# The backward bias of a relational graph layer: from the projections to the last means

## The chip, the cores and the metric

The kernel runs on one core of one Trainium2 chip. The metric is the time of one execution on the device in microseconds. The engines of the core are TensorE (PE; its weight loads are listed apart as PEld), VectorE (DVE), ScalarE (ACT), GpSimd (POOL) and SyncE (SP), which work side by side and wait for one another through semaphores.

## The reference

Two graph layers are applied to 3125 nodes of 256 features with 100000 edges: first an edge network with a gate (L0), then a relational layer (L1) with 16 relations, whose messages run along the edges and, with weights of their own, against them. The change concerns L1:

```
def _typed_pass(feat, W, bias, src_idx, dst_idx, etypes, norm_per_edge, n):
    proj = jnp.einsum('ni,rio->rno', feat, W)
    m = proj[etypes, src_idx] + bias
    m = m * norm_per_edge[:, None]
    return segment_sum(m, dst_idx, num_segments=n)
...
norm_f = _inv_degree(dst, n)[dst]
m_forward = _typed_pass(feat, Wf, forward_bias, src, dst, etypes, norm_f, n)
norm_b = _inv_degree(src, n)[src]
m_backward = _typed_pass(feat, Wb, backward_bias, dst, src, etypes, norm_b, n)
s = feat @ loop_weight
s = s + s + self_bias
return s + m_forward + m_backward
```

Since the norm of an edge is one over the number of edges of its node, each pass is a mean over a node's edges. The mean of a bias that is the same for all edges is the bias itself where the node has an edge, and 0 where it has none.

## The kernel before

Nodes lie in 25 blocks of 128 (`NB`), edges in 196 steps of 512 (`ST`, four columns of 128 edges). The program of each engine is written out by hand, in the order in which it runs; loops are hardware loops with 48 steps in a body.

**L0** (until some 1500 us of the profiled execution) computes the edge network step by step. Its second layer takes its bias by a product of ones with `bias_k` (`core_bias`, line 631), whose rows are made ready by `split_row` (lines 901 to 907).

**Forward projections** (some 1500 to 1812 us): relation pairs `q` = 0 to 7 multiply all 25 node blocks by two relations' weights. `project` (lines 766 to 778) makes six products of 128x512 for a block into one of five PSUM slots, ACT copies the slot (`evacuate`, line 264) and SP stores it to the table `proj` in HBM (line 325).

**The middle stage** (some 1867 to 3025 us) does two things at once. PE alternates between `project` for a block of the pairs 8 to 15, the backward weights (line 812), and `sum_projections` for a step of the forward sum (line 816). For the sum, POOL gathers four times 128 rows of `proj` per step (`gather_rows`, line 425) into one of eight buffers (`gbuf`), DVE compares the edges' nodes with the numbers of a node block (`one_hot`, line 1001), PE multiplies the two (line 679) and DVE adds the product to `acc` (`add_sums`, line 1034). Where a step's edges reach into further blocks, PE and DVE do a further round for each (lines 697 and 1025 to 1040). POOL may fill a buffer again when PE has reported the step that read it by `s_agg[1]` (line 434). In the first half of the stage DVE also sorts the edges by source (lines 1217 and 1220). In this stage alone `project` starts with a product of ones with the backward bias, which so stands in each projected row (lines 771 to 773).

**Between the stages** POOL waits until the last projection is stored (line 440), and DVE takes the forward means (`mean`, line 1279) and adds the forward bias (`forward_bias`, line 1284), times `some`, which is 1 for a node with edges and 0 otherwise. `fbias_p` is in PSUM.

**The last stage** (some 3027 to 4207 us) gathers from the backward projections into twelve buffers and sums by source over two blocks at once (`sum_backward`, line 721; `compare2`, `add2`, line 1058).

**The end**: `backward_mean` takes one over the number of edges and then 25 means, each of which reports to `s_final`; SP stores six blocks at a time, and the last 53 rows alone (lines 364 to 369).

Of the kernel before, what the change touches and what calls it, by code (L numbers as in the profile page):

```python
# [12 lines left out]
P = 128  # L13
# [13 lines left out]
NW = 12  # L27
# [24 lines left out]
def gnn_program(nc, x, dst_l, src_l, typ_l, ea_t, W1, b1, W2, b2, Wg, bg, gamma, beta,  # L52
# [9 lines left out]
    with ctx:  # L62
# [23 lines left out]
        bias_k = sb("bias_k", [P, 2, H], F32R)  # L86
# [3 lines left out]
        brow, gamma_b, beta_b = rows_a[:, 0:2 * H], rows_a[:, 2 * H:3 * H], rows_a[:, 3 * H:4 * H]  # L90
        rows_b = sb("rows_b", [P, 4 * H])
# [29 lines left out]
        bias_raw = fa[0:2, 6144:6144 + 2 * H].rearrange("p (d f) -> p d f", d=2)  # L121
# [104 lines left out]
        s_ones = sem("s_ones")  # L226
        s_xagg = [sem(f"s_xagg{k}") for k in range(3)]
# [67 lines left out]
        def _(sp):  # L295
# [66 lines left out]
            for n in range(5):  # L362
                sp.wait_ge(s_pst[n], 16 * 5 * NQ)
            for b in range(0, NB - 1, OB):
                sp.wait_ge(s_final, b + OB)
                sp.dma_start(out[b * P:(b + OB) * P, :].rearrange("(b p) f -> p b f", p=P), res[:, b:b + OB, :]).then_inc(s_out, 16)
# [81 lines left out]
        def _(act):  # L448
# [22 lines left out]
            for d, bias in enumerate((b2, bbias)):  # L471
                act.dma_start(bias_raw[:, d, :], bias.to_broadcast([2, H])).then_inc(s_w, 16)
# [115 lines left out]
        def _(pe):  # L588
# [177 lines left out]
            def project(q, u, b, d):  # L766

                n = b % 5
                if b >= 5 or past(q, 1):
                    pe.wait_ge(s_pev[n], 5 * q + b // 5)  # L770
                if d:
                    nc.tensor.matmul(pslots[n].rearrange("p (r f) -> p r f", r=2), ones_k[:, :],
                                     bias_k[:, 1:2, :].to_broadcast([P, 2, H]), start=True, stop=False)
                for m, (a, c) in enumerate(PARTS):
                    for kk in range(HK):
                        last = nc.tensor.matmul(pslots[n], hT[:, a, kk, b * P:(b + 1) * P], wsp[:, u, c, kk, :],  # L776
                                                start=(not d and m == 0 and kk == 0), stop=(m == 2 and kk == HK - 1))
                last.then_inc(s_proj, 1)

            def forward_relations(i):  # L780
                for u in range(2):
                    pe.wait_ge(s_wlo, 2 * i + u + 1)
                    for b in range(NB):
                        project(2 * i + u, u, b, 0)

            for g in range(NB // GB):
                for b in group(g):
                    transposes(1, b)
                if g == 0:
                    pe.wait_ge(s_wlo, 1)  # L790
                for b in group(g):
                    pe.wait_ge(s_hT[1], b + 1)
                    project(0, 0, b, 0)
            pe.wait_ge(s_wlo, 2)
            for b in range(NB):
                project(1, 1, b, 0)
# [9 lines left out]
            with pe.Fori(0, NQ // 4) as i:  # L806
                for u in range(2):
                    q = 2 * i + NQ // 2 + u
                    pe.wait_ge(s_wlo, q + 1)
                    project(q, u, 0, 1)  # L810
                    for m in range(QS):
                        project(q, u, m + 1, 1)
                        t = QS * u + m
                        if m % GS == 0:
                            w = windows_of(pe, 0, 2 * QS * i + GS + t, GS)
                        sum_projections(1, 2 * QS * i + GS + t, (GS + t) % RF, 2 * QS // RF * i + (GS + t) // RF, w[m % GS])
# [11 lines left out]
        def _(dve):  # L828
# [458 lines left out]
            def backward_mean():  # L1287

                inverse_degrees()
                for b in range(NB):  # L1290
                    mean(b, s_final)
# [107 lines left out]
```

## Time and profile before

| | us |
|---|---|
| median of 3 runs | 3757.14 |
| lowest, highest | 3756.84, 3758.55 |
| span of the profiled execution | 4225.8 |

The profiled execution is 468.7 us longer than the median of the runs. A row of a view is one group of instructions with its busy time and count; behind the bar or in square brackets is the time in which the engine sat idle just before them and what ended it. "issue" is idle time for which the profile shows no wait; "remote" is a wait whose end the profile cannot assign to an instruction. Starts of PE instructions are recorded, their ends are modelled.

### The profile page before, as it was taken

How to read it: one execution, taken by the hardware profiler on the slowest of the kernel's cores; microseconds unless marked ns; L12 is line 12 of the kernel's file. 1: busy time of each engine (PE TensorE's matmuls, PEld its weight loads, DVE VectorE, ACT ScalarE, POOL GpSimd, SP SyncE). 2: the span in 40 equal slices, each digit the busy share in tenths (PEclk: the TensorE clock that was granted, in tenths of full speed). 3: DMA queues.
4: the chain of work that ended last, by engine and by line, in shares of the span. 5: the costliest groups of instructions: out<-in, count | busy, mean ns of one | idle time of the engine just before them, and what ended most of it. 6: DMA issues, size and time to landing. Idle time of an engine off the chain costs nothing.

```text
span 4225.8 us, 72762 instructions
## 1 busy us (share of the span) xinstructions
PE 3453.7 (82%) x21136; PEld 2922.2 (69%) x21137; DVE 2451.8 (58%) x3368; ACT 984.1 (23%) x1538; POOL 2535.0 (60%) x3139
## 2 busy tenths in 40 slices
PE   6999999999999969966767777676668777778787
PEld 5989999989899958855555555565546565566655
DVE  6888888888888888845555532222423333333334
ACT  3444444544444444400111011001100000000000
POOL 2777777777777600046666666656566666666663
PEclk8999999999999989978888888889878888888888
DMA  5655655555555536634444464444333333333332
GB/s 166 171 168 163 171 169 163 168 163 166 164 165 161 153 106 204 207 120 134 141 140 141 126 148 141 138 128 133 103 90 91 89 87 87 88 88 92 92 91 80
DMA packets 322754, 569.98 MB, mean 135 GB/s; under 512 B 73896, under 2 KB 218392, under 8 KB 322584
## 3 DMA queue, kind: packets, MB, share of 16 engines
q0 software_dynamic: 137984, 411.19, 34.6%
q1 hardware_dynamic: 182732, 154.33, 11.4%
q10 hardware_dynamic: 1868, 2.52, 0.2%
q8 instruction: 67, 1.10, 0.1%
q14 instruction: 103, 0.84, 0.1%
HBM read 452.43 MB, written 115.41 MB: 134 GB/s over the span
## 4 chain that ended last, share of the span: by engine, by line
PE 47%; another core or an unknown queue 18%; issue 13%; DVE 12%; DVEq 7%; ACT 1%; POOL 1%; DMA 0%; POOLq 0%; ACTq 0%
PE pc L669 12%; PE pa L679 10%; PE pu L659 4%; DVE key L1220 4%; PE pg L643 4%; DVE tops L1217 3%; PE pu L651 3%; PE pu L721 3%; PE pa L721 2%; PE pg L721 2%; DVEq L277 2%; PE pu L776 1%; PE pg L776 1%; DVE fa L1001 1%
## 5 line engine op out<-in xcount | busy, mean ns | idle before, releaser
L406 POOL DMA_INDIRECT fa<-ptab,slot x784 | 814.1, 1038 | 348.8 <-issue 185.8
L425 POOL DMA_INDIRECT hr<-proj,row_dst x784 | 746.8, 953 | 427.6 <-issue 216.3
L425 POOL DMA_INDIRECT fa<-proj,row_src x400 | 381.5, 954 | 566.1 <-DMA proj<-fa 342.8
L669 PE MATMUL pc<-ws,hr 128*128 128x256 f32 x4704 | 614.4, 286 | 8.3 <-issue 6.7
L669 PEld LDWEIGHTS pc<-ws,hr 128*128 128x128 f32 x4704 | 577.3, 190 | 15.9 <-issue 15.0
L721 PE MATMUL pu<-hr,fa 128*128 128x258 f32 x1056 | 322.1, 441 | 134.5 <-issue 104.8
L679 PE MATMUL pa<-fa,onehot 128*128 128x256 f32 x904 | 252.3, 430 | 160.6 <-DVE onehot L1001 77.7
L721 PEld LDWEIGHTS pu<-hr,fa 128*128 128x128 f32 x1056 | 226.2, 217 | 214.7 <-issue 152.6
L1034 DVE TENSOR_TENSOR acc<-acc,pa 128x256 f32 x196 | 82.3, 420 | 465.9 <-remote 270.0
L679 PEld LDWEIGHTS pa<-fa,onehot 128*128 128x128 f32 x904 | 188.7, 214 | 213.4 <-issue 139.4
L721 PE MATMUL pg<-hr,fa 128*128 128x258 f32 x1040 | 301.0, 440 | 42.0 <-issue 39.2
L721 PEld LDWEIGHTS pg<-hr,fa 128*128 128x128 f32 x1040 | 231.2, 225 | 106.9 <-issue 64.1
L1001 DVE SCALAR_TENSOR_TENSOR fa<-pc,base,src_f 128x1024 f32<-128x1024 f32 (+1 forms) x210 | 261.6, 1247 | 74.7 <-issue 66.0
L505 ACT ACTIVATE hr<-pu 128x512 fp32r<-128x512 f32 x392 | 213.0, 596 | 303.1 <-PE pu L659 181.3
L516 ACT CAST hr<-fa 128x1024 fp32r<-128x1024 f32 x196 | 205.9, 1051 | 320.7 <-DVE fa L1008 249.4
L985 DVE SCALAR_TENSOR_TENSOR hr<-pu,hr 128x1024 fp32r<-128x1024 f32 x196 | 238.8, 1218 | 61.7 <-ACT hr L505 55.8
L721 PE MATMUL pa<-hr,fa 128*128 128x258 f32 x1040 | 252.4, 392 | 16.5 <-issue 15.2
L1008 DVE TENSOR_TENSOR fa<-fa,pc 128x1024 f32<-128x1024 f32 x196 | 238.1, 1215 | 44.2 <-PE pc L669 31.8
L776 PE MATMUL pu<-hr 128*128 128x512 f32 x960 | 256.1, 410 | 6.5 <-issue 5.2
L679 PE MATMUL pa<-hr 128*128 128x258 f32 (+1 forms) x1760 | 250.3, 285 | 11.6 <-issue 8.6
L1014 DVE TENSOR_TENSOR hr<-fa,hr 128x1024 fp32r<-128x1024 f32 x196 | 241.9, 1234 | 22.6 <-ACT hr L516 4.9
L425 POOL DMA_INDIRECT ws<-proj,row_src x192 | 181.5, 945 | 113.3 <-issue 52.1
(162 smaller groups left out, 5813.7 us busy)
## 6 DMA issues: line engine op xcount, KB each, us to landing
proj<-fa SPq DMA_DIRECT2D x400, 256.0 KB
fa<-in_ea_t SPq DMA_DIRECT2D x196, 128.0 KB
fa<-ptab,slot POOLq DMA_INDIRECT x784
hr<-proj,row_dst POOLq DMA_INDIRECT x784
fa<-in_Wrel SPq DMA_DIRECT2D x32, 256.0 KB
ptab<-fa SPq DMA_DIRECT2D x25, 256.0 KB, 2.0
fa<-proj,row_src POOLq DMA_INDIRECT x400
ws<-proj,row_src POOLq DMA_INDIRECT x192
```

Source lines behind the costliest of these rows:

```text
L406: pool.indirect_dma_start(pbuf[:, n % 2, j, :], None, ptab[:, :], bass.IndirectOffsetOnAxis(ap=slot[:, n, j:j + 1], axis=0)).then_inc(s_ga ...
L425: pool.indirect_dma_start(buffer[:, j, 0:H], None, table, bass.IndirectOffsetOnAxis(ap=rows[:, J * s + j:J * s + j + 1], axis=0)).then_inc ...
L505: last = nc.scalar.activation(uT[:, par, 0, h, :, :].rearrange("p k e -> p (k e)"), pu[:, h, :], ACT.Relu)
L516: nc.scalar.copy(msg[:, par, 0, :, :], gate[:, par, :, :]).then_inc(s_mhi, 1)
L669: last = nc.tensor.matmul(pc[:, j, :], uT[:, par, a, j // 2, kk, j % 2 * P:(j % 2 + 1) * P], w2s[:, c, kk, :], start=False, stop=(j == jj ...
L679: last = nc.tensor.matmul(pa[:, bank, 0:width], keys[:, at, j, :], rows[:, j, :], start=(n == 0), stop=(n == len(todo) - 1))
L721: last = nc.tensor.matmul(out[:, 0:AW], keys[:, j, :], raw2[:, n, j, :], start=(j == 0), stop=(j == J - 1))
L776: last = nc.tensor.matmul(pslots[n], hT[:, a, kk, b * P:(b + 1) * P], wsp[:, u, c, kk, :], start=(not d and m == 0 and kk == 0), stop=(m = ...
L985: nc.vector.scalar_tensor_tensor(out=uT[:, par, 1, :, :, :].rearrange("p h k e -> p h (k e)"), in0=pu[:, :, :], scalar=0.0, in1=uT[:, par, ...
L1001: return nc.vector.scalar_tensor_tensor(out=out, in0=numbers.unsqueeze(1).to_broadcast([P, J, width]), scalar=base[:, bass.ds(b, 1)], in1= ...
L1008: nc.vector.tensor_tensor(gate[:, par, :, :], gate[:, par, :, :], pc[:, :, :], ALU.mult).then_inc(s_msg, 1)
L1014: nc.vector.tensor_tensor(msg[:, par, 1, :, :], gate[:, par, :, :], msg[:, par, 0, :, :], ALU.subtract).then_inc(s_mlo, 1)
```

## The change

The backward projections lose their bias product: `project` has no argument `d` any more, and all its calls are alike. The backward bias is not loaded as a row for a product; SP loads it for all 128 partitions into the first quarter of `rows_a` (`bbias_b`), behind `s_ones`, when the forward sums and means that used this memory are over. At the end `backward_mean` computes `some` from the backward counts, adds bias times `some` to each block of `res`, and takes the mean of a block two blocks later, behind a wait on `s_bterm`.

```
-        bias_k = sb("bias_k", [P, 2, H], F32R)
+        bias_k = sb("bias_k", [P, 1, H], F32R)
...
+        bbias_b = rows_a[:, 0:H]
...
-        bias_raw = fa[0:2, 6144:6144 + 2 * H].rearrange("p (d f) -> p d f", d=2)
+        bias_raw = fa[0:2, 6144:6144 + H].rearrange("p (d f) -> p d f", d=1)
...
+            sp.wait_ge(s_ones, 1)
+            sp.dma_start(bbias_b, bbias.to_broadcast([P, H])).then_inc(s_bbias, 16)
             for b in range(0, NB - 1, OB):
...
-            for d, bias in enumerate((b2, bbias)):
-                act.dma_start(bias_raw[:, d, :], bias.to_broadcast([2, H])).then_inc(s_w, 16)
+            act.dma_start(bias_raw[:, 0, :], b2.to_broadcast([2, H])).then_inc(s_w, 16)
...
-            def project(q, u, b, d):
+            def project(q, u, b):
...
-                if d:
-                    nc.tensor.matmul(pslots[n].rearrange("p (r f) -> p r f", r=2), ones_k[:, :],
-                                     bias_k[:, 1:2, :].to_broadcast([P, 2, H]), start=True, stop=False)
                 for m, (a, c) in enumerate(PARTS):
                     for kk in range(HK):
                         last = nc.tensor.matmul(pslots[n], hT[:, a, kk, b * P:(b + 1) * P], wsp[:, u, c, kk, :],
-                                                start=(not d and m == 0 and kk == 0), stop=(m == 2 and kk == HK - 1))
+                                                start=(m == kk == 0), stop=(m == 2 and kk == HK - 1))
...
             def backward_mean():
 
+                nc.vector.tensor_scalar(some[:, :], acc[:, :, H], 1.0, None, ALU.min)
                 inverse_degrees()
-                for b in range(NB):
-                    mean(b, s_final)
+                dve.wait_ge(s_bbias, 16)
+                for b in range(NB + 2):
+                    if b < NB:
+                        nc.vector.scalar_tensor_tensor(out=res[:, b, :], in0=bbias_b, scalar=some[:, b:b + 1],
+                                                       in1=res[:, b, :], op0=ALU.mult, op1=ALU.add).then_inc(s_bterm, 1)
+                    if b >= 2:
+                        dve.wait_ge(s_bterm, b - 1)
+                        mean(b - 2, s_final)
```

On PE, in the loop of the middle stage, this stands before the change at the second block of a relation pair, with the sum of a step around it:

```order
731 L696 UNCONDITIONAL_BRANCH
732 L770 REGISTER_ALU
733 L772 MATMUL pu<-bias_k,ones_k 128x512 [waits s_pev0]
734 L776 MATMUL pu<-hr 128x512 x6
735 L277 ISA
736 L277 TENSOR_LOAD win
```

The same engine and loop after the change, at the third of the five slots:

```order
677 L700 UNCONDITIONAL_BRANCH
678 L777 MATMUL pg<-hr 128x512 [waits s_pev2]
679 L777 MATMUL pg<-hr 128x512 x5
680 L690 REGISTER_ALU
681 L694 REGISTER_ALU [waits s_add1,s_gath1_5,s_oh1]
```

The bias product is gone, and the wait for a free slot stands on the first product of the block.

On DVE, at the end of the program, before the change:

```order
2814 L1155 TENSOR_SCALAR inv<-acc 128x25 [waits s_add2,s_xadd2]
2815 L1156 RECIPROCAL inv<-inv 128x25 [waits s_dve]
2816 L1279 SCALAR_TENSOR_TENSOR res<-acc,inv,res 128x256 [waits s_dve]
2817 L1279 SCALAR_TENSOR_TENSOR res<-acc,inv,res 128x256 x24
2818 L62 UNCONDITIONAL_BRANCH
```

And after it:

```order
2814 L1290 TENSOR_SCALAR some<-acc 128x25 [waits s_add2,s_xadd2]
2815 L1156 TENSOR_SCALAR inv<-acc 128x25
2816 L1157 RECIPROCAL inv<-inv 128x25 [waits s_dve]
2817 L1295 SCALAR_TENSOR_TENSOR res<-rows_a,some,res 128x256 [waits s_bbias,s_dve]
2818 L1295 SCALAR_TENSOR_TENSOR res<-rows_a,some,res 128x256 x2
2819 L1280 SCALAR_TENSOR_TENSOR res<-acc,inv,res 128x256 [waits s_bterm]
2820 L1295 SCALAR_TENSOR_TENSOR res<-rows_a,some,res 128x256
2821 L1280 SCALAR_TENSOR_TENSOR res<-acc,inv,res 128x256 [waits s_bterm]
```

There are 25 instructions of 128x256 more, taken in turn with the means, and one small one.

## Rows read from the trace of the kernel before

**Rows 1.** The page: the span, then POOL's busy tenths and PE's granted clock in 40 slices.
```profile
span 4225.8 us, 72762 instructions
...
POOL 2777777777777600046666666656566666666663
PEclk8999999999999989978888888889878888888888
```

**Rows 2.** Busy time by stretch: start:end, length, busy us (instructions) per engine, PEclk, DMA.
```profile
100.00:1400.00 1300.00, 1267.06 (x12230) 1179.69 (x12229) 1131.76 (x1321) 633.54 (x915) 969.36 (x1460) 1.00 0.59 166
1600.00:1800.00 200.00, 198.73 (x870) 162.57 (x870) 175.19 (x261) 88.41 (x151) 0.00 (x0) 1.00 0.62 206
1869.00:2449.00 580.00, 412.47 (x1526) 323.25 (x1524) 315.14 (x506) 60.01 (x102) 368.98 (x389) 0.86 0.46 136
2449.00:3025.00 576.00, 419.21 (x1628) 336.34 (x1627) 143.91 (x250) 61.10 (x104) 347.29 (x366) 0.86 0.48 134
3100.00:4175.00 1075.00, 834.09 (x3041) 650.73 (x3041) 368.79 (x397) 0.00 (x0) 693.24 (x734) 0.84 0.31 90
```

**Rows 3.** Groups of POOL in the middle stage, 1869 to 3025 us, with idle time before them.
```profile
L425 POOL DMA_INDIRECT fa<-proj,row_src x384 | 366.4, 954 | 216.9 <-issue 104.3 <-PE pa L679 61.1 <-remote 51.5
L425 POOL DMA_INDIRECT ws<-proj,row_src x185 | 174.9, 945 | 95.7 <-issue 50.3 <-remote 30.1 <-PE pa L679 15.4
L425 POOL DMA_INDIRECT rows_b<-proj,row_src x92 | 86.9, 945 | 48.8 <-issue 24.3 <-remote 18.5 <-PE pa L679 6.0
L425 POOL DMA_INDIRECT rows_a<-proj,row_src x92 | 86.9, 945 | 56.0 <-issue 23.9 <-remote 19.2 <-PE pa L679 12.9
```

**Rows 4.** In order of time, middle stage: start, us, engine, line, what, idle before.
```profile
2619.68 1.89 PE L679 MATMUL pa<-fa,onehot 128*128 128x256 f32 x8
...
2621.21 0.58 PE L772 MATMUL pu<-bias_k,ones_k 128*128 128x512 f32 x1
...
2621.64 1.55 PE L776 MATMUL pu<-hr 128*128 128x512 f32 x6
...
2623.43 0.94 POOL L425 DMA_INDIRECT rows_b<-proj,row_src  x1 [2.01 <-remote]
...
2624.68 0.95 POOL L425 DMA_INDIRECT rows_b<-proj,row_src  x1 [0.30 <-issue]
```

**Rows 5.** Groups of the whole execution: the bias product, the means, the forward bias.
```profile
L772 PE MATMUL pg<-bias_k,ones_k 128*128 128x512 f32 x80 | 51.2, 640 | 0.0
...
L1279 DVE SCALAR_TENSOR_TENSOR res<-acc,inv,res 128x256 f32<-128x256 f32 x50 | 20.0, 479 | 0.1
...
L1284 DVE SCALAR_TENSOR_TENSOR res<-pc,some,res 128x256 f32<-128x256 f32 x25 | 9.9, 475 | 0.0
```

**Rows 6.** In order of time, end of the middle stage.
```profile
3000.07 0.94 POOL L425 DMA_INDIRECT fa<-proj,row_src  x1 [0.30 <-issue]
...
3000.56 0.99 PE L772 MATMUL pc<-bias_k,ones_k 128*128 128x512 f32 x1
...
3021.40 0.59 PE L772 MATMUL pc<-bias_k,ones_k 128*128 128x512 f32 x1
...
3026.95 0.97 POOL L425 DMA_INDIRECT hr<-proj,row_dst  x1 [24.50 <-DMA proj<-fa]
...
3050.42 5.46 PE L721 MATMUL pu<-hr,fa 128*128 128x258 f32 x16 [25.32 <-DVE hr L1336]
```

**Rows 7.** In order of time, the end of the program (L1155 is the degree's clamp).
```profile
4208.43 0.18 DVE L1155 TENSOR_SCALAR inv<-acc 128x25 f32<-128x25 f32 x1
...
4209.00 9.98 DVE L1279 SCALAR_TENSOR_TENSOR res<-acc,inv,res 128x256 f32<-128x256 f32 x25
...
4219.03 0.48 SPq L368 DMA_DIRECT2D out<-res  x1
```

**Rows 8.** In order of time, the start of L0: DVE's bias rows and PE's first wait.
```profile
80.77 0.74 DVE L906 SCALAR_TENSOR_TENSOR bias_k<-fa,ident,bias_k 2x512 fp32r<-2x512 f32 x1
...
82.69 0.48 DVE L906 SCALAR_TENSOR_TENSOR bias_k<-fa,ident,bias_k 2x256 fp32r<-2x256 f32 x1
...
86.97 1.97 PE L659 MATMUL pu<-ident,fa 128*128 128x128 f32 x8 [6.11 <-DMA fa<-ptab,slot]
```

## What the change should do to the time

> **What bounds the kernel now.** I read the slices of the page first, then the busy time by stretch, then the waits of the stages that the change touches, and last the rows in order of time at their ends. L0 keeps PE busy for 1267 of 1300 us and the forward projections for 199 of 200 us, both at full clock [rows 2]; the change leaves the work of both alone. The other half of the span is two gather stages. In the middle stage PE is busy for 412.5 + 419.2 = 832 of 1156 us at a granted clock of 0.86, and in the last one for 834 of 1075 us at 0.84 [rows 2]. No engine fills either. What goes on steadily there is POOL: its slices stand at 5 to 6 tenths [rows 1], but a gather of 0.95 us is followed by 0.30 us of "issue", so that one starts every 1.25 us [rows 4]. 784 of them make 980 of the 1156 us. POOL's idle time in the middle stage is 216.9 + 95.7 + 48.8 + 56.0 = 417 us; 203 us of it are issue, 95 us are waits for PE's sums (line 679), and 119 us are "remote" [rows 3]. Each wait of POOL that can last is the one for a free buffer, which PE's report of a finished sum ends, so the remote ones are of that kind too. The reader is to see in [rows 4] that such a wait can be long after the work: POOL goes on at 2623.43, while PE's recorded sum of 2619.68 is long over and PE has gone on to the next projection. So in this execution gathers and late reports set the pace; the number of products PE has to run matters only where PE is really behind.
>
> That the sort does not matter to the pace says the same: DVE is busy for 315 us in the first half of the stage and for 144 us in the second, and the two halves take 580 and 576 us [rows 2].
>
> **What the change removes from PE.** 25 blocks times 8 pairs are 200 bias products. Their mean duration is 640 ns [rows 5], which would be 128 us, but the record of a product that follows the sum begins while the sum is still running. The spacing tells the price. From the first product of the sum at 2619.68 to the first of the projection at 2621.64 are 1.96 us; the sum's eight records take 8 x 0.215 = 1.72 us of it, so the bias product takes 0.24 us [rows 4]. The plain stretch of projections gives the same: 870 products of the same width in 200 us, 0.23 us each [rows 2]. I take 0.227 us, in all 45 us, and at the mean clock of 0.86 at most 45 / 0.86 = 53 us. The Trainium skill, "TensorE: Matmul & The Clock Gate", section "Wait — 56ns, not 53.3ns?", gives 512 / 2.4 GHz + 2.5 ns = 216 ns from start to start when warm. By it the removed work would be an estimated 43 us, and the duration in the profile is no price; the spacing agrees.
>
> **How much of it reaches the end.** At least 0: POOL's gathers would take as long as before, and PE would only wait longer for them. At most 53 us: every product on the path. In between, the saving counts while POOL stands still for PE, which is (95 + 119) / 1156 = 0.19 of the stage [rows 3]. 0.19 x 45 is 8.4 us. I take this value; it is nearer to the lower bound since part of the remote waits ends by a late report and not by PE's work. The ends, 0 and 53, stay for the range.
>
> **The drain of the middle stage.** POOL's last gather starts at 3000.07, and its first backward gather must wait until the last projection is stored, 3026.95, a wait of 24.5 us [rows 6]. In that time PE works off what it is behind; six bias products stand there, from 3000.56 to 3021.40 [rows 6]. Here POOL waits for PE in full, so that 6 x 0.23 = 1.4 us go. PE itself starts the last stage at 3050.42, behind DVE's means and forward bias [rows 6], and would start 1.4 us earlier too.
>
> **What the change adds at the end.** DVE gets 25 instructions of 128x256 that multiply by a scalar and add, as the forward bias does: 9.9 us for 25 [rows 5]. The 25 last means take 9.98 us [rows 7], 0.40 us each. Nothing stands beside them: the sums are over, the outputs wait for the means, and the last store is issued right behind the last mean, at 4219.03 [rows 7]. So 25 x 0.40 = 10.0 us are on the path. The clamp for `some` is like the one of 0.18 us [rows 7]; together 10.2 us. The waits on `s_bterm` ask for an instruction that has two bias instructions and two means behind it or nearly so; at 0.40 us each the 0.48 us of an instruction are over by then, and I cost them at nothing. Were that cover gone, each of 25 waits would cost up to 0.1 us, 2.5 us in all. The Trainium skill, "Perfetto Trace Analysis", section "Optimizing Scalar/DVE Operations", says that instructions carry a fixed overhead, some 60 ns on SBUF and 125 ns on PSUM, and that grouping helps. By it reading the bias from SBUF instead of PSUM would save an estimated 25 x 65 ns = 1.6 us; the rows of L1279 and L1284, 479 and 475 ns, show no such difference.
>
> **What is moved and costs nothing.** The load of the bias on SP stands behind the wait for DVE's `s_ones`, which is set at about 3050 us; behind it on SP's queue are only the output stores, which wait for the last means, after 4209 [rows 7]. 128 KB have over 1100 us to land, and if that cover were gone it would be one load of some microseconds. At the start two rows are split instead of three: the four instructions on 2x512 become 2x256, for the last of them 0.74 us becomes 0.48 us [rows 8], for all four under 1 us. PE waits there for the first gather until 86.97 us, DVE's bias rows are over at 83.17 us [rows 8]; nothing is gained. A smaller first clearing of `bias_k` and one small load less on ACT's queue are costed at nothing for the same reason.
>
> **The sum.** + 10.2 - 1.4 - 8.4 = + 0.4 us on the profiled span of 4225.8 us, which is 4226.2 us. I carry the difference over to the median, 3757.14 + 0.4 = 3757.5 us. That step is the weak one: the runs are 468.7 us shorter than the profiled execution, and where the difference lies I cannot see.
>
> **Rivals.**
>
> First, PE paces the middle stage in the timed runs. L0 and the forward projections leave PE no idle time, so the 468.7 us must have gone from the gather stages for the most part. 1568 gathers times 0.30 us of issue are 470 us, which would be just the difference. Then a stage lasts 1156 - 235 = 921 us, and PE's 832 us are 90% of it instead of 72%. For it speaks this sum; against it, that some of POOL's gap must be real, and that PE at 90% would wait less and hold its full clock better. If half to all of the removed work counts, 23 to 53 us, the middle is 38 us, and the time is 3757.1 + 10.2 - 1.4 - 38 = 3728 us; the span of this case is 3713 to 3743 us.
>
> Second, slower: POOL's chain of gathers has no gap that PE's work makes, the drain and the end alone count. The mechanism is the 50 instructions at the end in place of 25, with PE's saving spent in longer waits for gathers. It decides as soon as the middle stage gives back less than 1.3 us: 3757.1 + 10.2 - 1.4 = 3766 us, or 3767 us with no saving in the drain. For it speaks that most of POOL's stops look alike, some 2 us, and end long after PE's recorded work [rows 4]; against it, the 95 us of waits that end with PE's sum itself [rows 3].
>
> Third, slower by the clock: PE is at the lower of its two levels, 1.2 instead of 2.4 GHz, for about 0.14 / 0.5 = 28% of the stage [rows 2], in stretches that follow PE's waits. With less to do between two gathers it waits more. If the mean fell from 0.86 to 0.84, 832 us of work would take 20 us more, and if all of that counted the time would be 3767 + 20 = 3787 us. The Trainium skill, "TensorE: Matmul & The Clock Gate", section "HAM oscillation — how this bites in real kernels", warns of it: gaps in PE's work let the clock fall back, and each burst begins cold. Only where PE is the pace can this cost, and there the gaps are short, so I give it little.
>
> That the change does not do what it says can be left out: the product is gone from PE's order, and the 25 instructions stand at DVE's end.
>
> **How the numbers follow.** The forecast, a part of the saving that about pays for the end, 0.38; PE as the pace, 0.36; nothing back in the middle, 0.21; the clock, 0.05. The time is that of the forecast, whose own range is 3750 to 3764 us (middle saving of 2 to 16 us). A measurement of this kernel can tell some 0.2%, 7.5 us, from no change. The first rival is faster by more than that, with 0.02 from the forecast's edge: 0.38. The second and third are slower, though a tenth of the second ends just inside: 0.24. Within 0.2%: 0.38. The range reaches down to 3720 us, which leaves out 0.08 of the first rival, and up to 3768 us, which leaves out the clock and the worst of the waits on `s_bterm`.
>
> **What would show it.** In the profile of the changed kernel the end from the last sum to the last store should be 10 us longer, with 50 instructions at a pace of 0.40 us; a longer pace means that the waits count. The middle stage from the first to the last sum should be 1 to 20 us shorter, with PE's busy time down by 45 to 130 us depending on how the first product's record is drawn; POOL should still start a gather every 1.25 us. If its waits for buffers shrink by more than 20 us, the first rival is right; if they stay and PE's waits grow by the whole saving, the second. A granted clock below 0.84 in the middle stage speaks for the third. A time under 3743 us with the profile's stages unchanged would mean that the profiled execution is paced by something that the timed runs lack, and the prediction rests on the wrong execution.

## The result and the profile after

The changed kernel takes 3767.26 us (median of 7 runs, 3764.74 to 3768.93), the kernel before 3757.14 us beside it (7 runs, 3755.33 to 3758.75). The ratio is 1.0025, with a 95% interval of 1.0014 to 1.0036: 10 us slower. The forecast was 3757.5 us.

One thing has to be known before any row is read. The kernel before has a median of 3757 to 3759 us on some chips (the first kind below), and of about 4225 us on others (the second kind), where no single run is under 4205 us. By its span of 4225.8 us the profiled execution of before belongs to the second kind; the timed runs, and the profile of the changed kernel, belong to the first. So the rows of after are set against another execution of the kernel before, taken on a chip of the first kind (e1_before, below), and not only against [rows 1 to 8].

The page of the changed kernel (span, POOL's busy tenths and PE's granted clock in 40 slices), for [rows 1]:

```profile
span 3765.5 us, 72389 instructions
...
POOL 1777777777777770002777777777777777777774
PEclk8999999999999998999888999999989999999998
```

The same of the kernel before, on a chip of the first kind:

```profile
span 3754.6 us, 72762 instructions
...
POOL 1777777777777770002777777777777777777775
PEclk8999999999999998999999999999989999999999
```

Where [rows 1] had POOL at 5 to 6 tenths in both gather stages, it stands at 7 in both kernels here. Busy time by stretch, after (columns as in [rows 2]: the two halves of the middle stage, then the last stage):

```profile
1781.00:2263.00 482.00, 371.30 (x1437) 291.31 (x1436) 313.81 (x511) 61.77 (x103) 364.93 (x385) 0.92 0.56 165
2263.00:2746.00 483.00, 374.43 (x1512) 293.26 (x1512) 145.35 (x250) 61.58 (x103) 363.30 (x383) 0.95 0.59 163
2800.00:3730.00 930.00, 713.28 (x3083) 570.04 (x3082) 378.04 (x397) 0.00 (x0) 703.55 (x743) 1.00 0.36 105
```

And e1_before, the whole middle stage and the last:

```profile
1784.00:2747.00 963.00, 770.16 (x3151) 608.00 (x3149) 459.08 (x760) 123.09 (x206) 727.15 (x766) 0.96 0.58 164
2800.00:3730.00 930.00, 716.01 (x3098) 572.92 (x3097) 379.61 (x399) 0.00 (x0) 703.33 (x745) 1.00 0.37 105
```

PE's busy time in the middle stage falls from 770 to 371.3 + 374.4 = 746 us. The stage does not get shorter. Two of POOL's groups in the middle stage of after, for [rows 3]:

```profile
L430 POOL DMA_INDIRECT fa<-proj,row_src x384 | 365.0, 950 | 117.1 <-issue 115.5 <-PE pa L683 1.5
L430 POOL DMA_INDIRECT ws<-proj,row_src x191 | 182.2, 954 | 58.2 <-issue 57.3 <-PE pa L683 0.9
```

and the same groups in e1_before:

```profile
L425 POOL DMA_INDIRECT fa<-proj,row_src x384 | 364.6, 949 | 117.0 <-issue 113.0 <-PE pa L679 4.0
L425 POOL DMA_INDIRECT ws<-proj,row_src x190 | 181.3, 954 | 57.9 <-issue 56.0 <-PE pa L679 1.8
```

117 us of idle time over 384 gathers is 0.30 us each. There is no other idle time: the 119 us of "remote" in [rows 3] are absent, and the waits for PE, 95 us there, are 4.0 + 1.8 us in these two groups of before and 1.5 + 0.9 us in those of after, none of them longer than the usual 0.3 us between two gathers. POOL starts a gather every 1.25 us from end to end, with the bias products and without them. From its first gather of the stage to its last are 984.3 us in e1_before (1754.39 to 2738.73) and 985.0 us after (1752.03 to 2737.00). What PE saved, it waits. The waits of PE in the middle stage (us in total, times, longest), e1_before:

```profile
PE pa L679 <- DVE onehot L1001: 89.4, 56, 8.1
PE pa L679 <- issue: 75.5, 59, 2.8
PE pa L679 <- DMA fa<-proj,row_src: 18.9, 14, 2.3
```

and after:

```profile
PE pa L683 <- DVE onehot L1002: 124.9, 69, 8.1
PE pa L683 <- issue: 59.3, 41, 3.1
PE pa L683 <- DMA fa<-proj,row_src: 20.4, 11, 2.7
```

Together 184 us before and 205 us after, nearly the difference of 24 us in busy time. That they go by the name of the one_hots does not make DVE the pace, since the gathers do not slow down.

The end of the program, after, in order of time, for [rows 7]:

```profile
3737.45 0.69 DVE L1059 TENSOR_TENSOR acc<-acc,pu 128x516 f32 x1 [4.32 <-PE pu L725]
3738.24 0.18 DVE L1290 TENSOR_SCALAR some<-acc 128x25 f32<-128x25 f32 x1
...
3738.90 1.28 DVE L1295 SCALAR_TENSOR_TENSOR res<-rows_a,some,res 128x256 f32<-128x256 f32 x3
3740.09 0.48 DVE L1280 SCALAR_TENSOR_TENSOR res<-acc,inv,res 128x256 f32<-128x256 f32 x1
3740.49 0.48 DVE L1295 SCALAR_TENSOR_TENSOR res<-rows_a,some,res 128x256 f32<-128x256 f32 x1
...
3757.51 1.27 DVE L1280 SCALAR_TENSOR_TENSOR res<-acc,inv,res 128x256 f32<-128x256 f32 x3
3758.83 0.40 SPq L373 DMA_DIRECT2D out<-res  x1
```

and of e1_before:

```profile
3736.46 0.69 DVE L1058 TENSOR_TENSOR acc<-acc,pu 128x516 f32 x1 [4.32 <-PE pu L721]
...
3737.82 9.99 DVE L1279 SCALAR_TENSOR_TENSOR res<-acc,inv,res 128x256 f32<-128x256 f32 x25
...
3747.86 0.48 SPq L368 DMA_DIRECT2D out<-res  x1
```

From the last sum's add to the end of the span are 3765.5 - 3737.45 = 28.05 us after, and 3754.6 - 3736.46 = 18.14 us before, 9.9 us less. The add itself comes at the same time within 1 us. The loss of 10 us is the end, and nothing has paid for it.

### The profile page after: what moved, and what is told of

It reads as the page before. It is cut to its first block, busy times and chain, and to the rows that moved or that the text cites. A ratio compares the mean times of both kernels' runs of the same rounds, so it can differ in the third digit from the quotient of the medians.

```text
span 3765.5 us, 72389 instructions
## 1 busy us (share of the span) xinstructions
PE 3198.4 (85%) x20936; PEld 2743.7 (73%) x20937; DVE 2468.0 (66%) x3394; ACT 994.1 (26%) x1538; POOL 2503.2 (66%) x3139
## 4 chain that ended last, share of the span: by engine, by line
PE 41%; POOL 30%; issue 13%; DVE 10%; DMA 1%; DVEq 1%; ACT 1%; POOLq 0%; ACTq 0%
POOL hr L430 18%; PE pc L673 14%; PE pa L683 9%; POOL fa L430 5%; PE pu L663 5%; PE pg L647 4%; DVE tops L1218 4%; DVE key L1221 4%; PE pu L655 3%; POOL ws L430 3%; POOL rows_b L430 1%; POOL rows_a L430 1%; PE pc L635 1%; PE pu L777 1%; DVE onehot L1002 1%
## 5 line engine op out<-in xcount | busy, mean ns | idle before, releaser
L411 POOL DMA_INDIRECT fa<-ptab,slot x784 | 776.1, 990 | 323.8 <-issue 255.7
L673 PE MATMUL pc<-ws,hr 128*128 128x256 f32 x4704 | 605.0, 284 | 0.0
L725 PE MATMUL pu<-hr,fa 128*128 128x258 f32 x1056 | 247.0, 386 | 83.7 <-issue 44.9
L725 PE MATMUL pg<-hr,fa 128*128 128x258 f32 x1040 | 241.6, 384 | 67.0 <-issue 52.5
L725 PE MATMUL pa<-hr,fa 128*128 128x258 f32 x1040 | 241.4, 384 | 64.1 <-issue 53.5
L725 PEld LDWEIGHTS pu<-hr,fa 128*128 128x128 f32 x1056 | 196.8, 190 | 132.3 <-issue 59.2
L777 PE MATMUL pu<-hr 128*128 128x512 f32 x960 | 268.7, 426 | 14.6 <-issue 13.9
L725 PEld LDWEIGHTS pg<-hr,fa 128*128 128x128 f32 x1040 | 192.7, 189 | 114.1 <-issue 68.7
L725 PEld LDWEIGHTS pa<-hr,fa 128*128 128x128 f32 x1040 | 192.8, 189 | 110.6 <-issue 70.0
L777 PE MATMUL pg<-hr 128*128 128x512 f32 x960 | 260.2, 414 | 0.0
```

The costliest lines, as they stand in the source:

```text
L411: pool.indirect_dma_start(pbuf[:, n % 2, j, :], None, ptab[:, :], bass.IndirectOffsetOnAxis(ap=slot[:, n, j:j + 1], axis=0)).then_inc(s_ga ...
L673: last = nc.tensor.matmul(pc[:, j, :], uT[:, par, a, j // 2, kk, j % 2 * P:(j % 2 + 1) * P], w2s[:, c, kk, :], start=False, stop=(j == jj ...
L725: last = nc.tensor.matmul(out[:, 0:AW], keys[:, j, :], raw2[:, n, j, :], start=(j == 0), stop=(j == J - 1))
```

## Experiments

My theory after the result: the chain of gathers paces both stages, PE's work is covered by it, and only what stands behind the last add counts. Rivals: the removed products do save something that another part of the change gives back; or PE's cover is thin, and the result hangs on the chip.

**The kernel before, again.** e1_before is the kernel before, unchanged.

> The kernel before, unchanged, for a second profile. Theory (POOL's gathers pace both gather stages, and the first profiled execution was held up by something that the timed runs lack): the span is near 3755 us, a gather starts every 1.25 us with no stop for a buffer, PE's granted clock in the middle stage is above 0.9. Rival (the kernel before really has POOL's 80 stops, and the change took them away): the span is again well over 4000 us in the profile, with stops of some 2 us after every 12 gathers. The timed runs: 3757 us by both.

It took 3759.68 us beside 3759.31, ratio 1.0002 (0.9993 to 1.0011). Its rows are those above. Its span, 3754.6 us, is 471 us shorter than that of [rows 1 to 8]. Much of this lies in POOL's stops, in the last stage as in the middle one. First POOL's gathers of that stage in the trace of [rows 1 to 8], then in e1_before:

```profile
L425 POOL DMA_INDIRECT hr<-proj,row_dst x784 | 746.8, 953 | 427.6 <-issue 216.3 <-remote 147.3 <-DMA proj<-fa 24.5
```
```profile
L425 POOL DMA_INDIRECT hr<-proj,row_dst x784 | 747.5, 954 | 241.9 <-issue 237.3 <-DMA proj<-fa 3.4 <-PE pu L721 0.6
```

A gather takes as long on both chips, 953 and 954 ns. The stops between them differ by 186 us. The starts of POOL's gathers divide the 471 us: the first gather of the middle stage comes at 1754.39 us here and at 1812.66 there, 58 us; from it to the stage's last gather are 984 and 1187 us, 203 us; from that to the first gather of the last stage (2744.48 here, 3026.95 in [rows 6]) the difference is 21 us, and behind it 189 us. So 413 us lie in the gather stages and 58 us ahead of them, in L0 for the most part. The stretch of L0 in e1_before, against the first of [rows 2]:

```profile
100.00:1400.00 1300.00, 1296.14 (x12782) 1222.68 (x12781) 1185.10 (x1382) 669.07 (x955) 976.17 (x1525) 1.00 0.62 173
```

PE issues 12,782 instructions in the 1300 us in place of 12,230, 4.5% more.

Where the stops of the second kind come from can be followed further in the trace of [rows 1 to 8]. In order of time, in its last stage:

```profile
3152.75 3.72 PE L721 MATMUL pg<-hr,fa 128*128 128x258 f32 x16
...
3156.31 3.65 PE L721 MATMUL pa<-hr,fa 128*128 128x258 f32 x16
...
3159.80 0.60 PE L721 MATMUL pu<-hr,fa 128*128 128x258 f32 x2
...
3162.78 1.11 PE L721 MATMUL pu<-hr,fa 128*128 128x258 f32 x4 [1.52 <-issue]
...
3167.04 2.79 PE L721 MATMUL pu<-hr,fa 128*128 128x258 f32 x5 [1.02 <-issue]
3167.99 0.69 DVE L1058 TENSOR_TENSOR acc<-acc,pg 128x516 f32 x1 [8.79 <-remote]
3168.01 0.95 POOL L425 DMA_INDIRECT hr<-proj,row_dst  x1 [2.62 <-remote]
```

The 16 products of the sum that starts at 3159.80 take 10.0 us, with four gaps inside it, 3.8 us in all, for which the profile shows no wait, and DVE gets to add the sum that PE began at 3152.75 only at 3167.99, at the moment at which POOL goes on. In the last stage of e1_before and of after each of the sums that I could follow takes 3.73 to 3.75 us, without a gap. So in this execution of the second kind PE halts and reports late, and POOL and DVE wait for it together.

**The end alone.** e2_end_only keeps the bias product and adds the change's load and its instructions behind the last sum, so that the bias is counted twice:

```
+                for b in range(NB + 2):
+                    if b < NB:
+                        nc.vector.scalar_tensor_tensor(out=res[:, b, :], in0=bbias_b, scalar=some[:, b:b + 1],
+                                                       in1=res[:, b, :], op0=ALU.mult, op1=ALU.add).then_inc(s_bterm, 1)
+                    if b >= 2:
+                        dve.wait_ge(s_bterm, b - 1)
+                        mean(b - 2, s_final)
```

> The kernel before with the change's end alone: the bias product stays in the projections, and the 25 additions of the bias stand behind the sums as well (the bias is counted twice in the output). Theory: 3757 + 10.2 = 3767 us, all of the change's loss. Rival (the end costs more than its instructions, by waits on s_bterm or by later stores, and the missing product gives part of it back): 3775 us or more.

3768.67 us, ratio 1.0025 (1.0014 to 1.0035), 9.4 us over before. The end alone is as slow as the whole change, and as long in the trace: 3762.8 - 3734.72 = 28.1 us from the last add.

**The product alone.** e3_product_gone has the other half: no bias product, and the end of before.

```
-                if d:
-                    nc.tensor.matmul(pslots[n].rearrange("p (r f) -> p r f", r=2), ones_k[:, :],
-                                     bias_k[:, 1:2, :].to_broadcast([P, 2, H]), start=True, stop=False)
```

> The changed kernel without the additions at the end: the bias product is gone, and the backward bias is left out of the output. Theory: PE's 45 us are no one's wait, only the drain of the middle stage is shorter: 3755 to 3757 us. Rival (PE paces part of the middle stage): 3735 us or less, and the end would have to cost 30 us.

3759.73 us beside 3759.31, ratio 1.0001 (0.9992 to 1.0010). Removing 200 products from PE gives nothing, or at most 3 us by the interval. Its middle stage, over the stretch used for e1_before:

```profile
1784.00:2747.00 963.00, 738.40 (x2932) 580.35 (x2930) 459.28 (x760) 123.95 (x208) 727.45 (x763) 0.94 0.57 164
```

PE is busy for 32 us less, DVE and POOL do the same work in the same time. The granted clock falls from 0.96 to 0.94, as the third rival had it, and costs nothing, because PE is not the pace.

**How thick the cover is.** e4_products_5 issues the bias product five times, e12_products_10 and e5_products_10 ten times. Each product starts the slot anew, so nothing of the computation changes; the expectation of e12 says otherwise, and is mistaken in that.

```
-                    nc.tensor.matmul(pslots[n].rearrange("p (r f) -> p r f", r=2), ones_k[:, :],
-                                     bias_k[:, 1:2, :].to_broadcast([P, 2, H]), start=True, stop=False)
+                    for k in range(5):
+                        nc.tensor.matmul(pslots[n].rearrange("p (r f) -> p r f", r=2), ones_k[:, :],
+                                         bias_k[:, 1:2, :].to_broadcast([P, 2, H]), start=True, stop=(k < 4))
```

> The kernel before with five bias products for each block instead of one (each starts the group anew, so that the output is the same): 800 products of 0.227 us more, 182 us of PE work. Theory: PE's step grows from some 3.4 to 4.3 us and stays under the 5.0 us of four gathers: 3757 to 3765 us. Rival (PE paces part of the stage): at least a quarter of the 182 us shows, 3800 us or more.

3762.92 us, ratio 1.0012 (1.0002 to 1.0021). Middle stage of e4:

```profile
1784.00:2747.00 963.00, 912.97 (x3949) 746.72 (x3949) 457.73 (x757) 123.23 (x206) 727.72 (x764) 0.99 0.58 164
```

800 products more make PE busy for 143 us more, 95% of the stage, and POOL's pace is what it was: 986.2 us from the first gather of the stage to the last, in place of 984.3. Most of the 3.6 us may be the drain, the time between that last gather and the end of PE's work of the stage, which is 4.1 us longer; the profiled execution, the slowest of the ten, is 10 us longer than that of e1_before in all and does not show it more closely. The first gather of the last stage, in e1_before, after, e4 and e12:

```profile
2744.48 0.96 POOL L425 DMA_INDIRECT hr<-proj,row_dst  x1 [3.35 <-DMA proj<-fa]
```
```profile
2743.22 0.96 POOL L430 DMA_INDIRECT hr<-proj,row_dst  x1 [3.83 <-DMA proj<-fa]
```
```profile
2751.60 0.97 POOL L425 DMA_INDIRECT hr<-proj,row_dst  x1 [7.49 <-DMA proj<-fa]
```
```profile
2915.57 0.97 POOL L425 DMA_INDIRECT hr<-proj,row_dst  x1 [36.81 <-DMA proj<-fa]
```

In e1_before and after this wait is 3.4 and 3.8 us; PE is hardly behind when the gathers end, and has next to nothing to catch up. With five products it is 7.5 us, with ten 37 us.

> The kernel before with the bias product of each backward projection issued ten times in place of once, so that the output is another one: 1,800 more small products. It tells PE's cover apart from the chip. Theory (the gathers pace the kernel until PE's own work in a middle stage is longer than the gathers'): with five products PE was busy 913 of 963 us, 143 us more than with one, so nine more bring 770 + 321 = 1,091 us by busy time, or 770 + 409 = 1,179 us by the spacing of 0.227 us. Where the kernel before runs in about 3757 us the stage of 963 us then grows by 130 to 215 us, 3885 to 3975 us, ratio 1.034 to 1.058. Where it runs in about 4225 us the stage has 1,187 us and nearly all is covered, as 4250.9 us showed: ratio 1.004 to 1.009. Rival (PE's work counts in full wherever it lies): 4166 us on the first, ratio 1.11.

3935.92 us, ratio 1.0475 (1.0459 to 1.0491): 178 us more, near the middle of what the theory gave, and 231 us less than work that counts in full would cost. Its middle stage, and POOL's largest group there:

```profile
1785.00:2900.00 1115.00, 1100.39 (x4862) 916.34 (x4861) 450.00 (x741) 121.82 (x204) 722.67 (x760) 1.00 0.49 141
```
```profile
L425 POOL DMA_INDIRECT fa<-proj,row_src x384 | 366.1, 953 | 208.5 <-PE pa L679 115.3 <-issue 93.2
```

Now PE is busy for 1100 of 1115 us, and POOL's waits end with PE's sum: this is how it looks where PE is the pace. PE's shortest step, from the first product of one sum to that of the next with a projection between them, is 3.32 us in e1_before, 4.25 us with five products and 5.40 us with ten, so a product costs 0.23 us, and the step has outgrown the 5.0 us of four gathers. From the first gather of the stage to the last are now 1124.8 us, 140 us more than in e1_before, and the drain is 33 us longer. Together that is the whole difference of the two spans, 3928.5 - 3754.6 = 174 us.

The same kernel on a chip of the second kind, where before takes 4225.29 us:

> The kernel before with ten bias products for each block instead of one: 1800 products more, 409 us of PE work. Theory (POOL's gathers pace the stage until PE's step is longer than theirs): PE's step is 3.4 + 9 x 0.227 = 5.4 us, over the 5.0 us of four gathers, so that the time rises by 196 x 0.4 us = 80 us and by what the 24 further rounds add, 1.7 us or more each: 3860 to 3920 us. Rival (something else than PE and POOL paces the stage): the time stays under 3800 us.

4250.86 us, ratio 1.0060 (1.0039 to 1.0081). The expectation was written for a chip of the first kind, and the some 100 to 160 us more that it gave did not come: 26 us here for what costs 178 us there.

```profile
1858.00:3045.00 1187.00, 1135.89 (x4945) 937.75 (x4944) 460.18 (x757) 121.64 (x206) 715.52 (x754) 0.98 0.45 132
```

The 1,800 products fill time in which PE stood: from the first gather of the stage to the last are 1208.8 us, in place of 1187.4 us in the trace of [rows 1 to 8], and the wait in the drain is 36.0 us in place of 24.5. The second kind of chip gives more cover, not less.

**Gathers.** e6_three_gathers makes three gathers per step in the last stage in place of four, so that the fourth quarter of a buffer keeps what was in it (same chip as e5).

```
-                gather_rows(raw2[:, s % RS, :, :], proj[1][:, :], row_dst, s, s_gath[2][s % RS])
+                gather_rows(raw2[:, s % RS, :, :], proj[1][:, :], row_dst, s, s_gath[2][s % RS], J - 1)
```

> The kernel before with three gathers for each step of the last stage instead of four; the fourth quarter of a buffer keeps what was in it, so that a quarter of the backward messages is left out of the output. Theory: 196 gathers of 1.25 us go from a chain without gaps, 245 us, less what PE then holds up, since its sum of 3.5 us is near the 3.75 us of three gathers: 3510 to 3560 us. Rival (the sums, not the gathers, pace the last stage): 3700 us or more.

3975.20 us, ratio 0.9398 (0.9365 to 0.9431): 250 us less for 196 gathers, 1.28 us for each. PE's and DVE's work in that stage was untouched. The expectation's times were those of the other kind of chip; its difference, 197 to 247 us, was just exceeded. What 200 products could not do, 196 gathers do. For the last stage of the first kind this was not run; there the rows of e1_before, with a gather every 1.25 us and no stop, have to speak for it.

**The change on the other kind of chip.** e9_change is the changed kernel.

> The changed kernel once more, on whichever chip this comes to: two chips so far gave the kernel before in 3759 us and two profiles of 4226 us and a third chip's runs in 4225 us. Where the kernel before takes 3757 to 3760 us, theory: 10 us more, 3767 to 3770 us, the end alone. Where it takes 4225 us (PE's reports come late there and POOL stops for them), theory: the end's 10 us stay, and the saving in PE work counts little, since the stops wait for the report and not for the work: 4225 to 4240 us. Rival there: PE's shorter step comes through, 45 us or so, 4170 to 4200 us.

4225.91 us beside 4224.69, ratio 1.0003 (0.9986 to 1.0021). The interval is from 6 us faster to 9 us slower. The end is as long as on the other chip, 28.0 us from the last add at 4214.13 to the end of the span at 4242.1, so a few of them may be paid back by the products on such a chip, as the forecast had it; the spread of single runs, 4213 to 4244 us, does not let me say so. The first half of its middle stage and its largest group of gathers, against [rows 2, 3]:

```profile
1869.00:2449.00 580.00, 395.30 (x1412) 310.54 (x1413) 310.80 (x502) 60.11 (x101) 368.22 (x387) 0.82 0.46 136
```
```profile
L430 POOL DMA_INDIRECT fa<-proj,row_src x384 | 366.2, 954 | 230.4 <-issue 106.9 <-PE pa L683 67.9 <-remote 55.6
```

PE is busy for 395 in place of 412 us, and the waits of POOL are not smaller for it, 230 in place of 217 us. In this profile at least the gathers gained nothing from it. The other executions of the second kind say the same: from the first gather of the middle stage to the last are 1181.1 to 1195.8 us in the four with one bias product for each block (the trace of [rows 1 to 8], e6, e7, e10) and 1181.9 and 1189.7 us in the two without (e8, e9). That rules out the rival's 45 us, and not a few us.

**A better end.** If only what follows the last add counts, means should be taken before it. In e7_early_means, e10_early_means and e11_early_means (one kernel, on three chips) DVE takes the inverse degrees ahead of the last six steps and four means after each of the next steps, three after the fifth, for the blocks that no later window reaches; six means stay for the end. The stores go from the last block to the first.

```
+            inverse_degrees()
+            early = list(range(NB - 1, OB - 1, -1))
+            for m in range(HS):
+                ...
+                add2(ST - HS + m, (GS + m) % HS, w[m])
+                if early[4 * m:4 * m + 4]:
+                    with dve.If(open_blocks < 1):
+                        finish(early[4 * m:4 * m + 4])
```

> The kernel before, with 19 of the 25 last means taken between the last six steps, where DVE idles, when the windows of these steps show that blocks 6 to 24 are complete (the edges are sorted by falling source), and with the outputs stored from the last block down. Theory (the end is DVE's chain of instructions and one last store, with nothing beside it): 19 x 0.40 = 7.6 us less, and some 3 us less since the store of 53 rows is not the last any more: 3745 to 3751 us where the kernel before has 3757 to 3759. Rival (the means between the steps delay the sums): no gain, 3757 us or more.

> The kernel before with 19 of 25 last means taken between the last six steps and the outputs stored from the last block down, once more. Theory: the end from the last sum to the last store is 10 us shorter whatever the chip: 3747 to 3750 us where the kernel before takes 3757 to 3760 us, and about 4215 us where it takes 4225 us. Rival (the means between the steps delay the sums, which PE has in stock): no difference from the kernel before.

On chips of the second kind e7 takes 4214.25 us beside 4225.29, ratio 0.9983 (0.9967 to 0.9999), and e10 4221.24 us beside 4224.69, ratio 0.9991 (0.9976 to 1.0005). Both point the right way, and the second cannot be told from no change.

> The changed kernel with the same early end: the additions of the bias and the means of blocks 24 to 6 between the last six steps, eight instructions in a step. Theory (the change loses only because nothing stands beside its additions): of the 10 us 19 / 25 are hidden, so that it comes out 6 x 0.40 = 2.4 us over the kernel before with early means, 3747 to 3754 us, and more only if 3.2 us of DVE work in a step delay the sums. Rival (the additions cost elsewhere too): 8 us or more over it.

e8_change_early does the same with the bias terms and means of the changed kernel: 4214.23 us, ratio 0.9975 (0.9961 to 0.9989), on the chip of e7. With most of the end out of the way, the change is no longer measurably slower than the kernel before with the same end; the 2.4 us that were expected are too few to be seen among runs that spread by 15 to 26 us.

> The kernel before, with the last six steps of the last backward stage each dividing four finished blocks (blocks 24 down to 6, where no later window can reach them) and only six means behind the last sum; outputs stored from block 24 down. Theory (the end is paid by what stands between the last sum's add and the end of the program, and the gather chain paces everything ahead of it): 19 means of 0.396 us leave the end, 7.5 us, and up to 2.5 us more of the chain of stores, less 1 to 3 us by which the last adds come later. Where the kernel before runs in about 3757 us that gives 3747 to 3752 us, ratio 0.997 to 0.9985. Where it runs in about 4225 us the same 6 to 10 us lie within the noise, ratio 0.996 to 1.000. Rival (the means delay DVE's one_hots so that PE falls behind the gathers): no gain, ratio 1.000 to 1.002.

3751.53 us beside 3758.23, ratio 0.9982 (0.9973 to 0.9991): 6.7 us faster, the fastest that I have. The end of e11:

```profile
3731.39 1.67 DVE L1279 SCALAR_TENSOR_TENSOR res<-acc,inv,res 128x256 f32<-128x256 f32 x4
...
3734.88 1.27 DVE L1279 SCALAR_TENSOR_TENSOR res<-acc,inv,res 128x256 f32<-128x256 f32 x3
...
3736.88 3.73 PE L721 MATMUL pu<-hr,fa 128*128 128x258 f32 x16 [2.85 <-issue]
3740.85 0.69 DVE L1058 TENSOR_TENSOR acc<-acc,pu 128x516 f32 x1 [4.70 <-PE pu L721]
...
3742.45 2.46 DVE L1279 SCALAR_TENSOR_TENSOR res<-acc,inv,res 128x256 f32<-128x256 f32 x6 [0.24 <-DVE inv L1156]
```

From the last add to the end of the span are 3749.1 - 3740.85 = 8.3 us in place of 18.1. Nineteen means of 0.40 us make 7.5 us of this; the rest goes with the stores, whose order was changed in the same run. The last add comes 4.4 us later than in e1_before. Of these, 2.3 us are there before the first early mean (the 25th gather from the end starts at 3701.87 and 3699.62), so they belong to the other execution; the other 2 us arise in the last six steps, among the early means and stores.

## Why the prediction was right in its range and wrong in its middle

The time of 3767.26 us is inside the range of 3720 to 3768 us, 0.7 us from its edge, and it is there only because the range was made to hold the rivals: the sum gave + 0.4 us, and + 10.1 us were measured. The case that I held likeliest did not come; the second rival did, to which I had given 0.21, and its price of 3766 to 3767 us was right. By the bound of 0.2% that I set, the change is slower, which had 0.24.

**The end: right.** 10.2 us were predicted. The trace shows 28.05 - 18.14 = 9.9 us, the timed end alone 9.4 us. The 50 instructions run from 3738.90 to 3758.8, 0.40 us each, so the waits on `s_bterm` cost nothing. An operand in SBUF in place of PSUM brought nothing either: 0.48 us for each line.

**The middle stage, 8.4 us: the step that failed.** It took a share of POOL's idle time, (95 + 119) / 1156, as the share of PE's saving that would reach the end. What the runs showed in its place is nothing: the middle stage and the drain were to give 9.8 us together, and e3, which has only the product gone, is at + 0.4 us (3 us less to 4 us more). Two things were wrong with the step. The stops belong to chips of the second kind; on the one that is timed, POOL's waits for PE in the two largest groups were 5.8 us in all, and no longer than the gap between any two gathers. And even on the second kind the share says nothing of what ends the waits: in e9 they are as long without the products. I had read the sign in [rows 4], where POOL goes on long after the recorded sum, called it a late report, and still put a fifth of the saving down to it. The stage was misread in length too: its 784 gathers do not lie in 1156 us but in 1187 us, from 1812.66 on; the 1156 us of [rows 2] hold 755 instructions of POOL.

**The drain, 1.4 us: failed.** The 24.5 us of [rows 6] are 3.35 us on this chip, and 3.83 us after the change. In the execution of [rows 6] PE was behind, with six bias products after POOL's last gather; in e1_before one is left, at 2738.76 beside the gather of 2738.73. With no backlog there was nothing to remove. On the second kind it stays open: 25.2 us in e9 and 22.8 in e8, without the products, lie among the 24.5 to 27.4 us of executions with them, or just below.

**The price of a bias product: right.** 0.227 us by spacing were taken. The steps of e1_before, e4 and e12, 3.32, 4.25 and 5.40 us, give 0.23 us, and in after the shortest step is 3.09 us, 0.23 us less. The 0.215 us that I set for each record of the sum stand in no row, though, and the price does not hang on them. Busy time gives less, 143 / 800 = 0.18 us within the stage and 349 / 1800 = 0.19 us over the whole program (3567.7 us in e12 against 3218.4 us in e11 on the same chip): the kernels with more products run at a higher granted clock, 0.99 and 1.00 against 0.96, so that the rest of their work is shorter. The mean of 640 ns in [rows 5] would have meant 512 us for the 800 of e4.

**Carrying the difference to the median: the weak step, and weak as feared.** I noted 468.7 us between the profiled execution and the runs. That they had gone from the gather stages for the most part was right, 413 of 471 us; but a term worked out from waits of the second kind, 95 + 119 us, was carried to an execution that has none of them. The text named what it would mean, that "the prediction rests on the wrong execution", but only for a time that is too short.

**The first rival, 0.36: false.** That 1568 gathers times 0.30 us are 470 us was a coincidence. The 0.30 us between gathers are there at full pace, 117 us for 384 of them. They are real, and so the stage is 963 us and not 921 us long, and PE has 770 us or 80% to do and not 90%. The argument against it that I had written, that some of the gap must be real, held for all of it.

**The third rival, the clock.** Its first half happened, 0.96 to 0.94 in e3, at no cost.

**What stays open.** Why PE halts and reports late on some chips is not known, and nothing was tried on it. Nor do I know whether the change is neutral there: e9 excludes neither 0 nor 8 us.

## What to carry to other kernels

Before a saving on one engine is weighed by how often another waits for it, look at whether the waits end with its work; where they don't, as here, it is worth nothing, and an engine that is 80% busy behind a steady chain has time to give away: 143 us more work for PE cost 3.6 us. An edit that moves work from under such a chain to the stretch behind the last instruction of the chain pays in full, and an edit that moves it the other way gains: here 19 means moved before the last add, with the stores in another order, brought 6.7 us. And where the profiled execution is 12% longer than the timed runs, it is another machine as far as the argument goes; ask of each term whether it rests on what the two share.

## What the runs showed of the hardware

Four chips are known by number. The kernel before has medians of 3759.31 and 3758.23 us on two of them and of 4225.29 and 4224.69 us on the other two. Each was used in one session, so that the chip and the session are not told apart. The gathers of the last stage take 953 and 954 ns on both kinds; those of L0 take 1038 ns on the second and 988 on the first, and L0 goes 4.5% slower there. In the gather stages of the second kind PE halts inside a sum, 10.0 us in place of 3.7, DVE waits for its sums by up to 9.5 us in place of 3.9, and where POOL's stops are regular (3116 to 3324 us) every 12 gathers take 17.3 us in place of 15.0. PE's granted clock in the last stage is 0.84 there and 1.00 on the first kind, with PE busy for 78% and 77% of the time; its longest single wait is 13.0 us there and 1.8 us on the first kind. Single runs of the kernel before spread by 31 to 32 us on the second kind and by 3 to 9 us on the first, so that an effect of 10 us can be measured on one and hardly on the other.

On the first kind POOL starts indirect gathers of 128 rows every 1.25 us, 0.95 us of work and 0.30 us without a wait, 784 in a row in each of the two stages: with a PE that is 77% busy in the last, and 80% or, in e4, 95% busy in the middle one. No run brought them closer.
